# A decoder layer in five hand-ordered engine programs: first and last iterations as lists of their own, preparation in nine pieces, loads in another order

## The chip, the cores and the metric

The kernel runs on one core of one Trainium2 chip. The metric is the device time of one launch in microseconds (us), median of three runs. A TensorE clock share ("PEclk") of 1.00 is the full 2.4 GHz, 0.50 is 1.2 GHz.

## The reference

The inputs are x (32 batches of 256 tokens, 256 wide, float32), a context of the same shape and one cell number per token. The layer has three residual blocks, each ended by a layernorm:

```python
x = _layernorm(x + _L0_attn_ref(x, Wq, Wk, Wv, Wo), axis=-1)
x = _layernorm(x + _L0_xattn_ref(x, ctx, ctx, cell, ...), axis=-1)
x = _layernorm(x + _L0_ffn_ref(x, w_gate, w_up, w_down), axis=-1)
```

- Self-attention: 16 query heads and 4 key/value heads of 64, rotary embedding, scores of 256 x 256 with a linear position term, softmax, values, output projection Wo.
- Cross-attention: layernorms (with gain and bias) of x and the context, projections q, k, v, 16 heads of 16, each query window of 64 tokens against its own and the previous window, masked to earlier tokens of the same cell, softmax, values, another layernorm with gain and bias, output projection.
- FFN: activations rounded to 8 bits by the row's maximum, weights rounded to -1, 0, 1 times their mean magnitude, silu(gate) * up, rounded again, down projection.

## The kernel before

Five programs run side by side, one for each of SyncE (SP, all DMAs), TensorE (PE), VectorE (DVE), ScalarE (ACT) and GpSimd (POOL). Each batch's work is cut into some 90 **steps**. One list, `BODY` (line 66), gives the order of the steps for one iteration, each with a lag; in iteration `it` a step works on batch `it - lag` (lags 0 to 4), so work of up to five batches is mixed. Every engine walks through the same list and does its part of each step. Semaphores carry the dependences; their counts are worked out from batch and step (`at`, `landed`). `freed` gives what a step has to wait for before it may write its PSUM bank.

The main steps, by their names in the list (PE's part first, then what follows on other engines):

- `X`: x of a batch, transposed, is split into a rounded part x_hi (ACT, line 934) and a remainder x_lo (POOL, line 1019). `K`, `V`, `Q` project it (three matmuls for each product, line 364), DVE and POOL apply the rotation (lines 613 to 631, 1028). `kT`, `qT` transpose (line 352).
- `S` p (p = 0 to 7): scores of two heads (line 418); DVE adds the position term and takes the row maximum (line 641), ACT exponentiates (line 953), `R`: DVE's reciprocal (line 648) and POOL's normalisation (line 1037). `T` n (0 to 15): transposes of the probabilities (line 352), copied by ACT (line 960). `O` p: values (line 436). `W`: output projection (line 444); DVE adds x; `YS`: statistics and scaling.
- `NX`, `QX`, `QXT`: transposes of the normalised y, projection to the cross-attention's query `qx_tok` (line 370; DVE, then POOL at line 1060), transposes of it. `KP`, `VP`: keys and values from the transposed context `cT` (line 370), loaded by `load_ctxT` (line 305), which waits until KP and VP of the batch before have read it. `KXT` and `fill_kx` lay out the keys. `SX` s (0 to 3), `TX` s e, `OX` g: scores (lines 485, 492), exponentials (line 976), transposes and values (line 511). `BX`, `NO`, `PO`: back to tokens, output projection; `FS`, `X2`: layernorm (line 771).
- `QN`, `QC`, `XQ`, `G` n, `U` n, `HS`, `HC`, `HT`, `D`, `ZS`, `out`, `store`: FFN with its rounding, last layernorm (line 854) and the write of y.

Around the loop: SP increments 105 semaphores (line 282, all counters start above zero), then issues three first loads (the two halves of the projection weights and the rope table), then 15 more with all other constants, the FFN weights among them, and only then xT and the context of batch 0 (`run(0)`). DVE splits the projection weights into a rounded part and a remainder (lines 859, 862: four instructions). Each engine then does iteration 0, which holds batch 0's steps of lag 0 alone. Between iterations 0 and 1 stands the **preparation**: layernorm gains are multiplied into the cross-attention weights, their column means taken out and their biases turned into rows (lines 866 to 894, and matmuls at lines 577, 582 and following), the FFN weights' mean magnitudes and the three-valued weights are made (lines 868, 895 to 909), and `turned_bias` is copied (line 912). PE, ACT and POOL wait for `pre_dve`, a count of DVE's preparation instructions, before they go on to iteration 1. Iterations 1 to 4 are the fill, written out from the same list with the batches that don't exist left out; 5 to 31 are 27 rounds of a hardware loop; 32 to 35 are the tail, again from the same list.

```python
for it in range(FILL):
    run(it)
with act.Fori(0, LAST - FILL) as j:
    run(j + FILL)
for it in range(LAST, B + max(LAGS)):
    run(it)
```

Of the kernel before, what the change touches and what calls it, by code (L numbers as in the profile page):

```python
# [15 lines left out]
P = 128  # L16
# [39 lines left out]
    z_st=2, z_mv=2, z_eps=1, z_rstd=1, out_ready=1,  # L56
# [10 lines left out]
    (2, 'KXT'), (3, 'TX', 3, 1), (1, 'kT'), (4, 'out'), (0, 'load_xT'), (2, 'T', 13), (3, 'OX', 1), (1, 'S', 0),  # L67
    (2, 'R', 15), (1, 'R', 0), (3, 'BX', 0), (1, 'R', 1), (1, 'Q', 1, 2), (2, 'T', 14), (2, 'O', 6), (3, 'BX', 1),
    (3, 'OS'), (2, 'T', 15), (1, 'S', 1), (2, 'VP'), (2, 'O', 7), (1, 'T', 0), (1, 'R', 2), (3, 'NO'), (0, 'X'),
    (1, 'qT', 2), (1, 'T', 1), (3, 'PO'), (1, 'VC'), (3, 'FS'), (1, 'CS'), (1, 'load_ctxT'), (1, 'R', 3), (3, 'X2'),  # L70
    (3, 'QN'), (3, 'QC'), (1, 'S', 2), (2, 'W'), (3, 'XQ'), (2, 'YS'), (1, 'R', 4), (1, 'R', 5), (1, 'T', 2),
    (2, 'mask'), (0, 'K'), (2, 'NX'), (1, 'qT', 3), (3, 'G', 0), (3, 'U', 0), (1, 'T', 3), (1, 'S', 3), (1, 'O', 0),
    (1, 'load_xtok'), (1, 'load_cell'), (2, 'QX'), (1, 'R', 6), (3, 'G', 1), (3, 'U', 1), (3, 'HS', 0), (1, 'T', 4),
    (0, 'V'), (1, 'T', 5), (2, 'QXT'), (0, 'Q', 0, 1), (1, 'S', 4), (2, 'fill_kx'), (2, 'SX', 0), (3, 'HC', 0),
    (1, 'O', 1), (1, 'T', 6), (1, 'R', 7), (1, 'R', 8), (1, 'R', 9), (0, 'Q', 1, 1), (2, 'SX', 1), (1, 'KP'),
    (2, 'TX', 0, 0), (1, 'O', 2), (3, 'G', 2), (3, 'U', 2), (0, 'load_ctx'), (2, 'TX', 0, 1), (0, 'qT', 0),
    (1, 'T', 7), (2, 'TX', 1, 0), (3, 'G', 3), (3, 'U', 3), (2, 'load_vs'), (4, 'store'), (2, 'TX', 1, 1),
    (1, 'S', 5), (1, 'R', 10), (1, 'O', 3), (2, 'OX', 0), (1, 'T', 8), (3, 'HS', 1), (2, 'SX', 2), (0, 'qT', 1),
    (0, 'Q', 0, 2), (1, 'R', 11), (1, 'T', 9), (1, 'S', 6), (3, 'HT', 0), (3, 'HC', 1), (2, 'TX', 2, 0), (1, 'T', 10),
    (2, 'SX', 3), (1, 'O', 4), (3, 'HT', 1), (2, 'TX', 2, 1), (1, 'R', 12), (1, 'R', 13), (1, 'T', 11), (1, 'S', 7),  # L80
    (3, 'D'), (3, 'ZS'), (2, 'X1'), (1, 'R', 14), (1, 'O', 5), (2, 'TX', 3, 0), (1, 'T', 12),
]

# [26 lines left out]
def freed(sem, bank, step, it):  # L110
# [3 lines left out]
    while True:  # L114
# [8 lines left out]
        if it < 0:  # L123
            return sem[name], 1
# [1061 lines left out]
```

## Time and profile before

| | |
|---|---|
| median of 3 runs | 2415.59 us (2413.31 to 2416.63) |
| profiled execution | 2412.44 us |
| its span | 2410.6 us, granted clock 0.980 |
| PE busy | 2259.2 us (94%), 17643 instructions |
| DVE busy | 1878.8 us (78%) |
| ACT busy | 1554.5 us (64%) |
| POOL busy | 1220.5 us (51%) |
| loop, iterations 5 to 31 | 346.5 to 2231.4 us |

Busy times are shares of the whole span; they are averages over a start, a loop and an end with different limits, so the rows by stretch of time tell more than they do. The span begins with the first instruction; the run's time has 1.8 us around it. In the rows the TensorE clock is the mean of what was granted in the stretch.

### The profile page before, as it was taken

Reading aid. Unit: us, or ns where it says so; the run is one execution under the profiler, and the core shown is the slowest. Engines: PE = TensorE matmul, PEld = TensorE weight load, DVE = VectorE, ACT = ScalarE, POOL = GpSimd, SP = SyncE. Lnnn points to the kernel's source line nnn. Section 1 sums busy time; section 2 is a strip of 40 time slices with the busy share of each in tenths; the row PEclk is TensorE's granted clock in tenths of the full one; section 3 lists DMA queues with packets and bytes.
Section 4 is the critical chain, followed back from the end, with each engine's and each line's share of the span. In section 5 each row is a group of like instructions: output and inputs, shape, how many; then the busy total and the mean of one; then the engine's idle time right before and its main releaser. Section 6 shows DMA issues by size and latency. Waiting matters only on the chain. (4 is left out here: it accounts for less than half of the span.)

```text
span 2410.6 us, 61139 instructions
## 1 busy us (share of the span) xinstructions
PE 2259.2 (94%) x17643; PEld 1629.1 (68%) x17706; DVE 1878.8 (78%) x7997; ACT 1554.5 (64%) x4577; POOL 1220.5 (51%) x1422
## 2 busy tenths in 40 slices
PE   1589999999999999999999999999999999999974
PEld 1467777777776777777777777777777777677652
DVE  2656888888788888888888888788888878888765
ACT  0256676666667766667777666767666676776641
POOL 1254555555555555555554555555555555555421
PEclk9799999999999999999999999999999999999986
DMA  4010011111001111110011111001111100111000
GB/s 160 10 29 15 21 35 30 33 33 33 16 24 30 28 33 33 33 28 14 28 28 33 33 33 33 13 24 33 28 33 33 33 15 22 32 28 28 25 14 9
DMA packets 84439, 71.87 MB, mean 30 GB/s; under 512 B 18336, under 2 KB 79136, under 8 KB 84384
## 3 DMA queue, kind: packets, MB, share of 16 engines
q1 hardware_dynamic: 84384, 71.19, 10.4%
q8 instruction: 28, 0.46, 0.1%
q14 instruction: 27, 0.22, 0.0%
HBM read 45.98 MB, written 8.39 MB: 23 GB/s over the span
## 5 line engine op out<-in xcount | busy, mean ns | idle before, releaser
L953 ACT ACTIVATE prob<-prob,nmax 128x256 f32<-128x256 f32 x1024 | 508.7, 499 | 555.2 <-DVE nmax L641 555.2
L1037 POOL TENSOR_TENSOR prob<-prob,precs 128x512 f32<-128x512 f32 x512 | 524.5, 1040 | 455.3 <-DVE precs L648 455.3
L641 DVE CUSTOM_DVE_ANT_0 prob<-bank,alibi 128x256 f32<-128x256 f32 x1024 | 372.5, 420 | 103.7 <-PE bank L418 102.0
L976 ACT ACTIVATE px<-px,nmx 128x128 f32<-128x128 f32 x1024 | 313.2, 391 | 19.3 <-DVE nmx L733 19.3
L960 ACT COPY pT<-bank 128x512 f32<-128x512 f32 x512 | 299.1, 584 | 37.2 <-PE bank L352 32.0
L352 PE MATMUL bank<-ident,prob 128*128 128x128 f32 x2048 | 314.6, 276 | 7.2 <-ACT pT L960 4.7
L418 PE MATMUL bank<-kk,qq 64*128 64x256 f32 x2048 | 291.3, 403 | 0.9 <-ACT kk L941 0.9
L436 PE MATMUL bank<-pT,v_sb 128*64 128x256 f32 x2048 | 277.5, 392 | 1.8 <-ACT pT L960 1.8
L352 PEld LDWEIGHTS bank<-ident,prob 128*128 128x128 f32 x2048 | 235.7, 141 | 63.1 <-issue 27.0
L733 DVE CUSTOM_DVE_ANT_0 px<-bank,mask 128x128 f32<-128x128 f32 x1024 | 225.8, 285 | 14.7 <-PE bank L492 4.6
L444 PE MATMUL bank<-wo,oT 128*128 128x256 f32 x1024 | 229.5, 382 | 0.0
L364 PE MATMUL bank<-w_hi,x_hi 128*128 128x512 f32 (+1 forms) x512 | 190.7, 372 | 38.3 <-POOL x_lo L1019 34.6
L418 PEld LDWEIGHTS bank<-kk,qq 64*128 64x128 f32 x2048 | 176.7, 186 | 64.5 <-issue 48.7
L436 PEld LDWEIGHTS bank<-pT,v_sb 128*64 128x64 f32 x2048 | 124.1, 136 | 137.7 <-issue 97.8
L444 PEld LDWEIGHTS bank<-wo,oT 128*128 128x128 f32 x1024 | 192.0, 190 | 35.1 <-issue 10.3
L1028 POOL TENSOR_TENSOR qtok<-qtok,by_sin 128x512 f32<-128x512 f32 x128 | 163.5, 1277 | 103.1 <-DVE by_sin L631 102.9
L953 ACT ACTIVATION_READ_ACCUMULATOR prob<-prob,nmax 128x1 f32 x1024 | 193.5, 189 | 0.0
L364 PE MATMUL bank<-w_hi,x_lo 128*128 128x512 f32 (+1 forms) x512 | 173.8, 339 | 0.0
L364 PE MATMUL bank<-w_lo,x_hi 128*128 128x512 f32 (+1 forms) x512 | 173.7, 339 | 0.0
L352 PE MATMUL bank<-ident,px 128*128 128x128 f32 x1024 | 161.8, 281 | 4.7 <-ACT pTx L983 3.3
L983 ACT COPY pTx<-bank 128x512 f32<-128x512 f32 x256 | 149.6, 585 | 23.1 <-PE bank L352 23.1
L352 PEld LDWEIGHTS bank<-ident,px 128*128 128x128 f32 x1024 | 112.0, 142 | 51.7 <-issue 41.2
(187 smaller groups left out, 4404.7 us busy)
## 6 DMA issues: line engine op xcount, KB each, us to landing
xT<-in_xT SPq DMA_DIRECT2D x32, 256.0 KB, 2.8
ctxt<-in_ctx SPq DMA_DIRECT2D x32, 256.0 KB, 2.8
cT<-in_ctxT SPq DMA_DIRECT2D x32, 256.0 KB, 2.6
xtok<-in_x SPq DMA_DIRECT2D x32, 256.0 KB, 2.6
kx<-kxT SPq DMA_DIRECT2D x256, 32.0 KB, 2.0
vs<-vx SPq DMA_DIRECT2D x64, 128.0 KB, 2.8
out_y<-y SPq DMA_DIRECT2D x32, 256.0 KB, 2.6
cellk<-in_cell SPq DMA_DIRECT2D x32, 64.0 KB, 2.9
```

The costliest lines, as they stand in the source:

```text
L352: last = nc.tensor.transpose(bank[:, n * P:(n + 1) * P], src, ident[:])
L364: last = mm(to, xs[:, k, t * P:(t + 1) * P], ws[:, k, cols], start=i == 0, stop=i == KT * 3 - 1)
L418: last = mm(psum[SCORES[c]][:, q * L:(q + 1) * L], qq[half, u, m, q * P:(q + 1) * P], kk[half, p // 4, :], start=True, stop=True)
L436: last = mm(psum[bank][c * HD:(c + 1) * HD, 0:L], v_sb[:, k, g * HD:(g + 1) * HD], pT[:, p % 2, c, k, :], start=k == 0, stop=k == TT - 1)
L444: last = mm(psum[bank][:, t * D:(t + 1) * D], oT[:, k, t * P:(t + 1) * P], wo[:, k, :], start=k == 0, stop=k == PAIRS - 1)
L641: v.tensor_tensor_reduce(out=prob[:, (2 * p + q) % SLOTS, c, :], in0=psum[SCORES[c]][:, q * L:(q + 1) * L], in1=alibi[:, p % 2, c, :], sca ...
L733: v.tensor_tensor_reduce(out=px[:, s % 2, i, :], in0=psum[XSCORES[r]][:, h * P:(h + 1) * P], in1=mask[:, s % 2, :], scale=-1.0, scalar=3.0 ...
L953: nc.scalar.activation(prob[:, (2 * p + q) % SLOTS, c, :], prob[:, (2 * p + q) % SLOTS, c, :], ACT.Exp, bias=nmax[:, i:i + 1], scale=-1.0, ...
L960: nc.scalar.copy(pT[:, p % 2, :, :, q * P:(q + 1) * P].rearrange("p c k n -> p (c k) n"), bank[:].rearrange("p (c n) -> p c n", c=4)).then ...
L976: ins = nc.scalar.activation(px[:, s % 2, i, :], px[:, s % 2, i, :], ACT.Exp, bias=nmx[:, 8 * s + i:8 * s + i + 1], scale=-1.0)
L1028: g.tensor_tensor(qtok[:, t, :], qtok[:, t, :], by_sin[:, n % 2, :], ALU.add).then_inc(sem["rot_sum"], 1)
L1037: g.tensor_tensor(prob[:, n % SLOTS, :, :], prob[:, n % SLOTS, :, :], precs[:, 2 * n:2 * n + 2].unsqueeze(2).to_broadcast([P, 2, L]), ALU. ...
```

## The change

1. The list of steps is now three lists. `HEAD` gives all of iterations 0 to 4, with batch numbers in place of lags; `TAIL` all of 32 to 35; `BODY` is a new order for the loop, with lags that differ for some steps (XQ to G stay at 3; HT 1, D, ZS are at 4; VP stands ahead of KP of the next batch, six PE steps between them). `freed` goes by the place in the list.
2. The preparation is nine pieces ('prep', 0) to ('prep', 8) in `HEAD`. 0 are the four copies of the biases, 1 the bias matmuls, gain products and bias rows, 2 and 3 the turned biases and the centring, 4 `turned_bias`, 5 the sums of the FFN weights, 6, 7, 8 the three-valued weights, one matrix each. Piece 0 and 1 are ahead of batch 0's S 0, pieces 2 to 7 between its steps up to W, piece 8 behind its QXT.
3. SP issues its first loads, alibi among them, before the increments, then context and xT of batch 0, then the cross-attention constants ('loads', 0), Wo ('loads', 1) and, once the weights are split, the FFN weights ('loads', 2). These three groups have semaphores of their own.
4. The weights are split in twelve pieces of 512 columns. Staging buffers are other tiles (`pTx`, `hh`, `px`; `bwide` in `oT`).
5. DVE's X2 waits for y3_ready of the batch before, a wait that was not there.

```diff
 BODY = [
-    (2, 'KXT'), (3, 'TX', 3, 1), (1, 'kT'), (4, 'out'), (0, 'load_xT'), (2, 'T', 13), (3, 'OX', 1), (1, 'S', 0),
...
-    (0, 'V'), (1, 'T', 5), (2, 'QXT'), (0, 'Q', 0, 1), (1, 'S', 4), (2, 'fill_kx'), (2, 'SX', 0), (3, 'HC', 0),
...
+    (2, 'NX'), (3, 'G', 0), (3, 'U', 0), (2, 'QX'), (1, 'T', 4), (1, 'R', 7), (1, 'qT', 2), (3, 'G', 1), (3, 'U', 1),
+    (1, 'T', 5), (1, 'S', 4), (3, 'HS', 0), (3, 'G', 2), (1, 'O', 1), (3, 'U', 2), (1, 'T', 6), (0, 'V'), (1, 'R', 8),
+    (2, 'QXT'), (3, 'G', 3), (1, 'R', 9), (1, 'qT', 3), (3, 'U', 3), (1, 'T', 7), (1, 'S', 5), (2, 'fill_kx'),
+    (2, 'SX', 0), (1, 'O', 2), (0, 'Q', 0, 1), (2, 'VP'), (3, 'HC', 0), (1, 'T', 8), (1, 'R', 10), (1, 'CS'),
+    (1, 'R', 11), (2, 'TX', 0, 0), (2, 'SX', 1), (1, 'T', 9), (1, 'S', 6), (3, 'HS', 1), (1, 'O', 3),
+    (1, 'load_ctxT'), (1, 'KP'), (2, 'TX', 0, 1), (1, 'T', 10), (2, 'SX', 2), (1, 'O', 4), (2, 'TX', 1, 0),
...
+HEAD = [
+    (0, 'load_ctx'), (0, 'load_xT'), (0, 'loads', 0), (0, 'prep', 0), (0, 'loads', 1), (0, 'X'), (0, 'K'), (0, 'V'),
+    (1, 'load_xT'), (0, 'Q', 0, 1), (0, 'kT'), (0, 'Q', 1, 1), (0, 'CS'), (1, 'load_ctx'), (0, 'prep', 1),
+    (0, 'qT', 0), (0, 'qT', 1), (0, 'S', 0), (0, 'R', 0), (0, 'Q', 0, 2), (0, 'R', 1), (0, 'S', 1), (0, 'R', 2),
...
+    (0, 'R', 13), (0, 'S', 7), (0, 'R', 14), (0, 'KP'), (1, 'kT'), (0, 'T', 12), (0, 'T', 13), (0, 'R', 15),
+    (0, 'O', 5), (0, 'T', 14), (0, 'T', 15), (0, 'O', 6), (0, 'O', 7), (0, 'loads', 2), (0, 'prep', 5),
+    (0, 'prep', 6), (0, 'prep', 7), (1, 'S', 0), (1, 'R', 0), (0, 'VP'), (1, 'load_ctxT'), (0, 'load_xtok'), (0, 'W'),
...
+TAIL = [
...
+    (30, 'U', 0), (31, 'QX'), (30, 'G', 1), (30, 'U', 1), (31, 'QXT'), (31, 'mask'), (31, 'SX', 0), (31, 'TX', 0, 0),
+    (31, 'SX', 1), (31, 'VP'), (31, 'TX', 0, 1), (31, 'SX', 2), (30, 'G', 2), (30, 'U', 2), (31, 'load_vs'),
+    (30, 'HS', 0), (31, 'TX', 1, 0), (31, 'TX', 1, 1), (31, 'SX', 3), (30, 'HC', 0), (31, 'OX', 0), (31, 'TX', 2, 0),
...
+    (31, 'XQ'), (31, 'G', 0), (31, 'U', 0), (30, 'out'), (30, 'store'), (31, 'G', 1), (31, 'U', 1), (31, 'G', 2),
...
+def freed(sem, bank, part, n, it):
+    before = part[:n]
+    if part is BODY:
+        before = [(it - 1 - lag, *step) for lag, *step in BODY] + [(it - lag, *step) for lag, *step in before]
+    elif part is TAIL:
+        before = [(LAST - 1 - lag, *step) for lag, *step in BODY] + before
+    for batch, *step in reversed(before):
+        if holds(step[0], bank) or (step == ["prep", 5] and bank == 7):
...
         def _(sp):
+            for dst, src in first_loads:
+                sp.dma_start(dst, src).then_inc(proj_loaded, 16)
             for name, n in COUNT.items():
                 sp.sem_inc(sem[name], CREDIT * n)
...
+                    if kind == "loads":
+                        g, = args
+                        if g == 2:
+                            sp.wait_ge(pre_dve, W_SPLIT)
+                        for dst, src in later_loads[g]:
+                            sp.dma_start(dst, src).then_inc(later_loaded[g], 16)
...
+            def prepare(n, place):
+                crossed = (wkvx[:, :, 0:D], wqx, wkvx[:, :, D:2 * D], wox)
+                if n == 1:
+                    pe.wait_ge(later_loaded[0], 16 * len(later_loads[0]))
+                    pe.wait_ge(pre_dve, P_WIDE)
...
+                elif n == 5:
+                    pe.wait_ge(pre_dve, P_SUMS)
+                    pe.wait_ge(*freed(sem, 7, HEAD, place, 0))
+                    mm(psum[7][:, 0:3], ones, wsum[:], start=True, stop=True).then_inc(pre_pe, 1)
+                elif n == 8:
+                    pe.wait_ge(pre_dve, PRE_DVE)
...
+            def prepare(n):
...
+                elif n == 5:
+                    dve.wait_ge(later_loaded[2], 16 * len(later_loads[2]))
+                    for m in range(3):
+                        v.tensor_reduce(wsum[:, m:m + 1], stage[m], AX_X, ALU.add, apply_absolute_value=True).then_inc(pre_dve, 1)
...
                     elif kind == "X2":
+                        dve.wait_ge(*at("y3_ready", b - 1))
                         dve.wait_ge(*at("f_rstd", b))
...
-            for k in range(KT):
-                v.tensor_copy(w_hi[:, k, :], raw_w[k]).then_inc(pre_dve, 1)
...
+            for i in range(3):
+                cols = slice(512 * i, 512 * i + 512)
                 for k in range(KT):
+                    v.tensor_copy(w_hi[:, k, cols], raw_w[k][:, cols]).then_inc(pre_dve, 1)
...
-            run(0)
-            pool.wait_ge(pre_dve, PRE_DVE)
-            for it in range(1, FILL):
-                run(it)
+            run(HEAD)
```

How the instructions stand on three engines, before and in the change. First SP, from its first instruction. Before:

```order
L335 DMA hh<-in_wqkv 128x1536
L335 DMA pT<-in_wqkv 128x1536
L335 DMA rope<-in_rope 128x256
L337 DMA alibi<-in_alibi 128x1024
...
L337 DMA wo<-in_wo 128x8x256
...
L337 DMA brow<-in_b_o 128x256
L295 DMA xT<-in_xT 128x2x256
L301 DMA ctxt<-in_ctx 128x2x256
```

Now:

```order
L374 DMA hh<-in_wqkv 128x1536
L374 DMA px<-in_wqkv 128x1536
L374 DMA rope<-in_rope 128x256
L374 DMA alibi<-in_alibi 128x1024
L398 DMA ctxt<-in_ctx 128x2x256
L392 DMA xT<-in_xT 128x2x256
L389 DMA gb<-in_gb 128x16
L389 DMA wqx<-in_wqx 128x2x256
```

xT of batch 0 went from the nineteenth DMA to the sixth; the semaphore increments, which are no rows here, went from ahead of the first DMA to behind the fourth.

Then DVE, from batch 0's last projection step before its first score step (line 641 before, line 802 now). Before, with the rest of the preparation left out:

```order
L631 TENSOR_TENSOR by_sin<-bank,rope 128x8x32 x2
L866 COPY pTx<-gb 128x256 x4
L868 TENSOR_REDUCE wsum<-prob 128x1
L868 TENSOR_REDUCE wsum<-oT 128x1
L868 TENSOR_REDUCE wsum<-px 128x1
...
L909 TENSOR_SCALAR wd<-px 128x2048
L912 COPY turned_bias<-bank 128x512 x2
L641 ISA prob,nmax<-bank,alibi 128x256
```

Now:

```order
L792 TENSOR_TENSOR by_sin<-bank,rope 128x8x32 x2
L844 BN_STATS c_bn<-ctxt 128x6 x2
L848 BN_AGGR c_mv<-c_bn 128x2 x2
L706 TENSOR_SCALAR wkvx<-wkvx,gb 128x256 x2
L706 TENSOR_SCALAR wqx<-wqx,gb 128x256 x2
L706 TENSOR_SCALAR wkvx<-wkvx,gb 128x256 x2
L706 TENSOR_SCALAR wox<-wox,gb 128x256 x2
L708 TENSOR_TENSOR noT<-bank,noT 128x512
L708 TENSOR_TENSOR brow<-bank,brow 128x512
L802 ISA prob,nmax<-bank,alibi 128x256
```

Only piece 1 still stands between the projections and the first scores; the sums, centring and three-valued weights went behind them.

Last PE in the loop, around QXT, the transposes of qx_tok. Before:

```order
L352 MATMUL bank2<-ident,prob 128x128 x4
L352 MATMUL bank7<-ident,qx_tok 128x128 x4
L364 MATMUL bank3<-w_hi,x_hi 128x512
L364 MATMUL bank3<-w_hi,x_lo 128x512
L364 MATMUL bank3<-w_lo,x_hi 128x512
```

Now:

```order
L453 MATMUL bank3<-w_lo,x_hi 128x256
L441 MATMUL bank7<-ident,qx_tok 128x128 x4
L656 REGISTER_ALU
L658 MATMUL bank5<-wg16,xqT 128x512 x2
L522 REGISTER_ALU
L441 MATMUL bank4<-ident,qtok 128x128 x4
L668 MATMUL bank6<-wu16,xqT 128x512 x2
```

QXT stood behind two T steps and now stands behind V, with G 3, qT 3 and U 3 after it in place of a Q step.

## Rows read from the trace of the kernel before

**Rows 1.** Windows: us, then busy us (instructions) of PE, PEld, DVE, ACT, POOL; PEclk, DMA share, GB/s
```profile
0.00:34.60 34.60, 0.01 (x1) 0.04 (x1) 5.16 (x4) 1.90 (x2) 5.35 (x15) 1.00 0.72 252
34.60:53.60 19.00, 11.67 (x50) 8.67 (x50) 4.05 (x9) 1.78 (x3) 3.84 (x3) 0.93 0.16 48
53.60:63.70 10.10, 0.05 (x1) 0.01 (x1) 9.82 (x10) 0.00 (x0) 1.26 (x1) 0.50 0.00 0
63.70:93.20 29.50, 11.04 (x42) 8.76 (x42) 22.53 (x50) 0.00 (x0) 0.00 (x0) 0.73 0.00 0
95.00:154.70 59.70, 49.80 (x323) 34.26 (x323) 30.34 (x135) 37.10 (x115) 32.08 (x31) 0.97 0.05 14
346.50:2231.40 1884.90, 1871.69 (x14853) 1358.00 (x14906) 1552.70 (x6697) 1307.63 (x3862) 1026.81 (x1188) 1.00 0.10 28
2298.90:2361.00 62.10, 44.72 (x313) 28.71 (x314) 35.63 (x145) 22.42 (x55) 13.41 (x20) 0.84 0.06 14
2361.00:2410.60 49.60, 20.47 (x123) 11.00 (x124) 24.27 (x66) 4.51 (x7) 9.30 (x15) 0.61 0.03 11
```

**Rows 2.** Groups of SP's queue, line 330, at each loop end: first and last start
```profile
L330 SPq MOVE out_y<-y x27: 38/38/38, 385.4 to 2199.3; - x27
```

**Rows 3.** Start: groups (min/median/max ns), timeline (start, us, engine) and DMA issues
```profile
L282 SPq EVENT_SEMAPHORE  x105: 17/17/17, 0.7 to 7.3; - x105
...
25.54 0.43 SPq L295 DMA_DIRECT2D xT<-in_xT  x1
...
14.09 0.96 DVE L859 CAST w_hi<-hh 128x1536 fp32r<-128x1536 f32 x1 [14.09 <-DMA rope<-in_rope]
17.50 1.75 DVE L862 TENSOR_TENSOR w_lo<-pT,w_hi 128x1536 fp32r<-128x1536 f32 x1
...
32.37 0.62 ACT L934 CAST x_hi<-xT 128x512 fp32r<-128x512 f32 x1 [29.68 <-DMA xT<-in_xT]
...
xT<-in_xT SPq DMA_DIRECT2D x32, 256.0 KB, 2.8
alibi<-in_alibi SPq DMA_DIRECT2D x1, 512.0 KB, 6.5
```

**Rows 4.** Timeline of DVE in the preparation, first instruction for the three-valued weights
```profile
81.51 1.28 DVE L903 TENSOR_SCALAR prob<-prob,wrec 128x2048 f32<-128x2048 f32 x1
```

**Rows 5.** Last layernorm's scaling on DVE, its group; timeline of POOL at its first
```profile
L854 DVE TENSOR_SCALAR y<-y,z_mv,z_rstd x64: 407/651/670, 278.3 to 2407.7; 128x256 f32<-128x256 f32 x64
...
278.31 1.12 POOL L1054 TENSOR_SCALAR x<-y,y_negm,y_rstd 128x256 f32<-128x256 f32 x2
```

**Rows 6.** Timeline of PE's weight loads in one loop iteration
```profile
1052.53 0.47 PEld L352 LDWEIGHTS bank<-ident,prob 128*128 128x128 f32 x4
1053.16 0.73 PEld L418 LDWEIGHTS bank<-kk,qq 64*128 64x128 f32 x8 [0.17 <-issue]
1054.23 1.59 PEld L370 LDWEIGHTS bank<-wkvx,cT 128*128 128x128 f32 x8 [0.33 <-issue]
1056.15 0.63 PEld L436 LDWEIGHTS bank<-pT,v_sb 128*64 128x64 f32 x8 [0.33 <-issue]
...
1079.92 0.47 PEld L352 LDWEIGHTS bank<-ident,prob 128*128 128x128 f32 x4
1080.91 0.42 PEld L352 LDWEIGHTS bank<-ident,qx_tok 128*128 128x128 f32 x4 [0.52 <-POOL qx_tok L1060]
1081.29 0.19 PEld L364 LDWEIGHTS bank<-w_hi,x_hi 128*128 128x128 f32 x1
```

**Rows 7.** DMA issues: count, KB each, median us to landing
```profile
cT<-in_ctxT SPq DMA_DIRECT2D x32, 256.0 KB, 2.6
```

**Rows 8.** Timelines of PE and ACT: batch 31's SX 0, its second group's exponentials, OX 1
```profile
2331.27 2.08 PE L485 MATMUL bank<-kx,qx 64*128 64x512 f32 x4 [1.86 <-DVE qx L678]
...
2337.98 2.44 ACT L976 ACTIVATE px<-px,nmx 128x128 f32<-128x128 f32 x8 [1.67 <-DVE nmx L733]
...
2362.33 0.42 PE L511 MATMUL bank<-pTx,vx 128*32 128x128 f32 x8 [0.68 <-ACT pTx L983]
```

## Prediction of the change's time

> **What bounds the kernel now.** I read the windows by stage first [rows 1]. In the 27 loop iterations, from 346.5 to 2231.4 us, PE is busy 1871.69 of 1884.90 us, so the loop is bound by PE's own row of work; one iteration takes (2199.3 - 385.4) / 26 = 69.77 us by the loop-end marks [rows 2]. The ends are different. PE does nothing for the first 34.60 us. In 34.6 to 53.6 it projects batch 0. In 53.6 to 93.2, 39.6 us, the kernel prepares constants: PE is busy 0.05 + 11.04 us, ACT not at all, DVE 9.82 + 22.53 = 32.35 us, and the granted clock is 0.50 and then 0.73, the half-speed level (1.2 GHz) and a mixture with the full one. From 95.0, the first score step S0, to 154.7, where batch 0's W starts, PE is busy 49.80 of 59.70 us, DVE 30.34. At the other end, from 2298.9, PE is busy 44.72 of 62.10 and 20.47 of 49.60 us, at clocks of 0.84 and 0.61. So some 40 + 34 us at the start and 17 + 29 us at the end are waits that no PE work fills, and the loop has only 13 us of them. The change can win much at the ends, and in the loop only what PE loses between its instructions.
>
> **First part, loads and split.** The chain that ends the first wait is on SP. It makes 105 semaphore increments from 0.7 to 7.3, issues 18 DMAs, and only at 25.54 issues xT of batch 0; ACT's x_hi waits 29.68 us for it and starts at 32.37, and the first matmul comes at 34.60, 2.2 us behind x_hi's start [rows 1, 3]. Unqueued, an xT takes 2.8 us to land. Now the order has four DMAs first, then the increments, then ctxt and xT. The increments took 6.6 us, so xT is issued at about 0.7 + 6.6, plus some 2.7 for the five issues ahead of it (0.43 for one like it [rows 3], more for large ones), = 10.0, lands at 12.9, and x_lo is ready at 15.1. The weight split waits for alibi too: issued near 2.3, 6.5 us to landing, so 8.8; the split took from 14.09 to 17.50 + 1.75 = 19.25, 5.2 us, and I allow 0.7 more for the starts of eight further instructions, so it ends at 14.7. The first matmul goes to 15.1, bounds 14.7 (split alone) and 19 (xT queued behind the loads ahead of it: the old one was issued at 25.54 and landed only some 6.8 us later). Gain 19.5 us.
>
> **Second part, preparation.** Projections to S0 hold no preparation any more except pieces 0 and 1: 19.0 us of the old window, plus 93.2 to 95.0 (the kT step), less one projection of Q that now follows S0, about 3: 17.8 us. S0 comes at 15.1 + 17.8 = 33 instead of 95.0: -62 us. What was between must be done beside batch 0's attention. Of the 32.35 us on DVE, three ternary instructions of about 1.28 [rows 4], 3.8 us, are in the last piece, behind W; the other 28.5 us fall ahead of batch 0's W or ahead of S0. DVE is idle for 59.70 - 30.34 = 29.4 us of that stretch, so the bounds are 0 (all in idle time) and 28.5 (all on the path). The softmax of batch 0 runs in a chain through DVE, and the pieces are blocks of several microseconds that a score step must wait behind; but PE has 10 us of waits there already, and batch 1's projections now stand in them. I take 9, a third. The matmuls of the preparation, 11 us at a low clock, shrink towards 6 to 7 and are in PE's gaps. Start: -62 + 9 = -53 us.
>
> What DVE's pieces cost may be more than their old durations. The scaling of the last layernorm, two tensor_scalars of 128x256, took 407 ns each at the least and 651 at the median [rows 5]; and a POOL scaling starts at 278.31, at the same time as DVE's first at 278.3, so the longer ones are those beside POOL. Before, POOL had no instruction at all in the last 29.5 us of the preparation [rows 1]; now it normalises beside it. At 651 / 407 = 1.6, the tensor_scalars and copies in pieces 0, 1 and 8, about 8 us, would take 4.9 more; the ternary pieces 6 and 7 stand where POOL has little. All of it is in the 9 or hidden. The Trainium skill, page "SBUF — State Buffer", section "Who interferes with whom", says that DVE and GpSimd share one pair of ports under an exclusive lock, so that copies and tensor_scalars contend and reductions do not. That rule speaks against this change; with it added in full the sum would be 2324 instead of 2319, and the trace's 651 against 407 agrees with it.
>
> **Third part, the loop.** The steps are the same, so are the matmuls; only waits and the changes from one kind of step to another can differ [rows 6]. QXT (transposes of qx_tok) starts 0.99 us behind the transposes before it (1079.92 to 1080.91), where four transposes otherwise take 0.38 (1080.91 to 1081.29): 0.6 us of waiting for POOL's qx_tok. Between QX and QXT stood G1, U1, T4, V and T5; now also qT2, S4, G2, O1, U2 and T6 stand there, some 5 us more, so I count that as gone: -0.6. A step on the whole array ahead of one that uses half of its rows or columns costs 0.63 (1052.53 to 1053.16) instead of 0.38, so 0.25 more. The new list has 14 runs of such half-array steps instead of 15, and the two by-token steps VP and PO no longer stand directly in front of one (1.92 us from 1054.23 to 1056.15 for VP): -0.5. Against it stand places grown tight: NX to QX has only two FFN matmul pairs between, and G1 to G2 one transpose step, a score step and a tanh; +0.25. That makes -0.85 per iteration: 27 in the loop and 4 in the fill give 31 x -0.85 = -26 us. The bounds are 0 (each stall replaced by one of its size, 0.6 + 0.25) and -1.8 per iteration.
>
> VP and KP in the loop now share a short path: SP loads the next cT only when VP has read the last, and KP wants it. After VP's end come T8, TX, SX1, T9, S6 and O3: 0.38 + 0.63 + 0.63 + 1.07 (S, 1053.16 to 1054.23) and about 1 for each of SX1 and O3, some 4.7 us. A cT takes 2.6 us to land [rows 7] and 0.4 to issue: 1.6 us to spare. I cost it at nothing; the cover is those six steps. SP's queue is in order, but ahead of load_ctxT stand only fill_kx, long done by then.
>
> **Fourth part, the tail.** For the last batch PE goes from SX0 at 2331.27 to OX1 at 2362.33, 31.1 us [rows 8]. ACT's part in it is four groups of exponentials at 2.44 us and the copies, some 17 us; the rest is PE steps of FFN and waiting for scores that were asked for late. Now SX2 stands ahead of batch 31's OX0 and VP fills a gap, so I take 20: -11. The stretch ahead of W loses about 5. X2 of batch 31 now waits for y3 of batch 30, and out of 30 stands between U0 and U1: +2. Tail -14, bounds -4 and -24. Each list also holds other batches' steps than before (HEAD some 11 us less of PE, TAIL some 11 more); that cancels.
>
> **Sum.** -53 - 26 - 14 = -93 against the profiled execution of 2412.4: 2319.4. The median of the three runs, 2415.6, lies 3.2 above that execution; I give **2320**.
>
> **Rivals.**
> A, the forecast: 2303 to 2337. 0.59.
> B, the new loop order is better than counted: stalls and most changes of step vanish, 1.8 us per iteration; another 31 x -0.95 = -29: about 2291. For it: the loop's 0.7% idle is small, but weight loads show 0.1 to 0.5 us of stalls at many steps. Against: that is all that PE loses. 0.12.
> C, the loop gains nothing, each stall moved: +26, about 2346. For it: PE busy is 99.3%, so what a reorder can give is small and it may tighten others. 0.15.
> D, preparation pieces block the softmax chain of batch 0 to the full, made longer by POOL's traffic: 28.5 - 9 = +19.5 and up to 4.9: about 2341. For it: DVE makes each row maximum. Against: half of DVE's time there is idle. 0.08.
> E, slower than before: KP waits in each iteration for the cT that SP can issue only when VP is through. The start and tail win 67 us, so the loop would have to lose 2.5 us per iteration, on top of the 1.6 us to spare and of the 0.85 gained: the path VP, DMA, KP must be 5 us longer than 3.0 us, say because the landing takes 8 us beside the other loads. At 6 us of excess: -67 + 27 x 3.6 = +30, 2442. Nothing in the rows shows a cT so late. 0.04.
> F, the early S0 changes nothing later: batch 0 is waiting for the constants or for DVE until where it was, and the loop gives nothing: within 5 us of 2412. 0.02.
>
> **How the numbers follow.** The range takes in A to D: B's 2291 with its spread below, C's 2346 above: 2284 to 2350; outside are E, F and edges of B and D, some 0.15. About 0.2%, 4.8 us, is what a measurement of this kernel can tell from no change. Cases A to D are all faster by far more: 0.94; F is the same, 0.02; E slower, 0.04.
>
> **What would show it.** First matmul at 15 (19 would mean xT queued), S0 at 33, batch 0's W near 101, the loop entered about 67 us earlier (53, 3 of the fill's iterations, and the 11 of PE steps that went to the tail); loop period 68.9 by the loop-end marks; no wait of QXT on qx_tok; KP without a wait on cT; DVE's preparation pieces summing to 32 to 37 us; OX1 of the last batch some 20 us behind its SX0. I am wrong if S0 starts later than 40, if W(0) minus S0 is over 75 us (D), if the period is 69.7 or more (C) or below 68.3 (B), or if KP shows a wait of more than 1 us per iteration (E).

## The result and the profile after

The changed kernel takes **2455.54 us** (median of 4 runs, 2449.53 to 2456.05) against 2415.02 before: 1.0161 times as long, 95% interval 1.0146 to 1.0176. The forecast was 2320, with a range of 2284 to 2350 and 0.04 for slower. It was wrong in sign.

The windows by stage of the changed kernel, columns as in [rows 1]:

```profile
0.00:15.80 15.80, 0.00 (x0) 0.01 (x1) 5.71 (x12) 1.90 (x2) 5.78 (x15) 1.00 0.66 230
15.80:40.00 24.20, 15.70 (x64) 12.96 (x64) 7.48 (x24) 1.77 (x3) 4.83 (x5) 0.79 0.42 115
40.00:98.50 58.50, 49.80 (x316) 35.56 (x316) 44.97 (x144) 32.12 (x96) 27.23 (x25) 0.97 0.16 54
294.50:2273.10 1978.60, 1898.90 (x14906) 1392.20 (x14904) 1538.00 (x6699) 1319.67 (x3862) 1020.40 (x1186) 0.99 0.10 27
2403.00:2453.30 50.30, 24.16 (x132) 13.39 (x121) 26.52 (x75) 3.92 (x6) 8.56 (x15) 0.60 0.05 16
```

The first three rows are the start, and it went much as forecast: first matmul at 15.8 (34.6 before), S 0 of batch 0 at 40.0 (95.0), its W at 98.7 (154.7), with DVE busy 44.97 us of the last stretch instead of 30.34. The fourth row is the loop, and there the kernel lost: 1978.6 us for the same 27 rounds that took 1884.9, 79.7 us of them with PE idle, 13.2 before. The marks of the loop end give the period, as in [rows 2]:

```profile
L427 SPq MOVE out_y<-y x27: 29/29/29, 320.0 to 2228.3; - x27
```

(2228.3 - 320.0) / 26 = 73.40 us, against 69.77 before and 68.9 forecast.

To share the difference out I gave each PE step the shortest time that its kind took in the loop before, and compared the elapsed time of fill, loop and tail with the sum of the steps in them, since the three lists hold other steps than before. Beyond the steps' own time the fill took 132.9 us before and 90.9 after, -42.0; the loop 201.3 and 295.1, +93.8; the tail 81.1 and 71.9, -9.2. The sum, +42.6, is the difference of the spans but for rounding (2453.3 - 2410.6 = 42.7). PE's idle time, which needs no such account, says the same of the ends: 86.5 us before the loop and 43.9 after the change, 51.7 and 42.5 behind it.

Where the loop waits, the list of waits says only in part. The two that are new and large:

```profile
PE bank L441 <- ACT oT L1078: 58.8, 26, 2.7
DVE nmx L894 <- issue: 42.5, 26, 1.9
```

Line 441 is a transpose (here kT, which needs bank 4), line 894 the row maximum of SX. The first is 2.3 us per round, and was a wait that I had not looked for. The second is stranger: "issue" means that the engine waited for nothing that the profile shows. Here is the timeline of DVE at that place in one round, and ACT's behind it:

```profile
1248.16 0.27 DVE L809 RECIPROCAL precs<-psums 128x2 f32<-128x2 f32 x2 [1.37 <-ACT prob L1066]
1248.56 0.29 DVE L894 CUSTOM_DVE_ANT_0 px<-bank,mask 128x128 f32<-128x128 f32 x1
1250.67 0.08 DVE L894 DVE_READ_ACCUMULATOR2_ANT nmx<- 128x1 f32 x1 [1.82 <-issue]
1250.74 0.29 DVE L894 CUSTOM_DVE_ANT_0 px<-bank,mask 128x128 f32<-128x128 f32 x1
```
```profile
1247.65 0.58 ACT L1096 COPY pTx<-bank 128x512 f32<-128x512 f32 x1
1250.79 2.45 ACT L1089 ACTIVATE px<-px,nmx 128x128 f32<-128x128 f32 x8 [2.57 <-DVE nmx L894]
1253.14 0.35 ACT L1078 COPY oT<-bank 128x256 f32<-128x256 f32 x1
```

DVE stands still for 1.8 us between one instruction and the next one of the same SX 3. ACT's eight exponentials wait for it, ACT's copy of oT (O 5) is queued behind them, and kT on PE waits for that copy. SX 3 is the first thing in the new loop after three short ones. The page's list of DMA queues has the line that goes with it. After, and then before:

```profile
q14 instruction: 157, 1.29, 0.2%
```
```profile
q14 instruction: 27, 0.22, 0.0%
```

130 more packets of instructions, 5 for each of 26 rounds, each of 1.29 MB / 157 = 8.2 KB. In the trace they fall into the loop: round by round at -8.6, +1.0, +3.4, +5.8 and some +36 us from the branch at the end of DVE's loop. Before, there were none between the first round and the last. The same place shows what they cost. The loop's line, in the round above, has the branch back to its start (COMPARE_BRANCH) and the first register instruction that DVE runs behind it (FUSED_REGOPS):

```profile
L1030 DVEq COMPARE_BRANCH  x1: 68/68/68, 1245.1 to 1245.1; - x1
L1030 DVEq FUSED_REGOPS  x1: 74/74/74, 1248.0 to 1248.0; - x1
```

2.9 us lie between the two here, 2.85 in the mean of the 26 rounds; before, it was 0.28.

### The profile page after: what moved, and what is told of

Same layout as the page of the kernel before. It is cut to its first block and busy times, and to the rows that moved or that the text cites. A ratio compares the mean times of both kernels' runs of the same rounds, so it can differ in the third digit from the quotient of the medians.

```text
span 2453.3 us, 61410 instructions
## 1 busy us (share of the span) xinstructions
PE 2287.2 (93%) x17706; PEld 1662.5 (68%) x17706; DVE 1866.3 (76%) x8005; ACT 1568.6 (64%) x4577; POOL 1219.1 (50%) x1422
## 3 DMA queue, kind: packets, MB, share of 16 engines
q14 instruction: 157, 1.29, 0.2%
## 5 line engine op out<-in xcount | busy, mean ns | idle before, releaser
L441 PE MATMUL bank<-ident,prob 128*128 128x128 f32 x2048 | 320.1, 280 | 8.2 <-ACT pT L1073 7.0
L441 PEld LDWEIGHTS bank<-ident,prob 128*128 128x128 f32 x2048 | 243.4, 143 | 96.1 <-issue 55.7
L453 PE MATMUL bank<-w_hi,x_hi 128*128 128x512 f32 (+1 forms) x512 | 193.0, 377 | 23.7 <-POOL x_lo L1133 15.8
L441 PE MATMUL bank<-ident,px 128*128 128x128 f32 x1024 | 167.4, 288 | 18.3 <-ACT pTx L1096 15.6
L1207 POOL TENSOR_SCALAR hh<-hh,hs 128x1024 f32<-128x1024 f32 x64 | 71.7, 1121 | 212.2 <-DVE hs L987 212.2
```

The source lines that it names most:

```text
L441: last = nc.tensor.transpose(bank[:, n * P:(n + 1) * P], src, ident[:])
L453: last = mm(to, xs[:, k, t * P:(t + 1) * P], ws[:, k, cols], start=i == 0, stop=i == KT * 3 - 1)
```

## Theories

**F, loading of instructions:** DVE's loop doesn't stay in the engine's instruction buffer and is loaded again in each round, because of where in the program it begins. DVE's program has 974 instructions ahead of a loop of 339 before, and 951 ahead of 340 after. **O, the order:** the new order of the steps is worse by itself; it puts ACT's copy of O 5 behind the exponentials of SX 3. The forecast's own rival for "slower", a late cT, was out at once: PE has no wait on cT.

## Experiments

**1. More instructions ahead of DVE's loop**, 64 of them.

```diff
+            for _ in range(64):
+                dve.sem_inc(waits_passed, 1)
             dve.wait_ge(proj_loaded, 16 * len(first_loads))
```

> The changed kernel with 64 more instructions at the very start of DVE's program (semaphore increments that nobody waits for, made while DVE waits for the loads), nothing else. In the trace of the change, queue q14 moved 157 packets of instructions where before it moved 27, 130 more, 5 for each of 26 loop rounds, and DVE stands still for 1.2 us at its loop end and for 1.55 to 1.9 us behind the first instruction of SX 3 with no wait to blame. Theory F (DVE's loop is loaded anew in every round, because of where in the program it begins; before it began elsewhere): q14 falls back to about 27 packets, both stalls are gone, the wait of kT for bank 4 shrinks from 2.5 to about 0.8 us, the period goes from 73.3 to 71.5 or a little lower, the time to about 2405. Theory O (the order of the new loop is to blame: the copy of O 5 stands behind the eight exponentials of SX 3 on ACT): period stays at 73.3 within 0.3 us and the time at 2455, even if q14 falls.

Measured: 2404.23 us, 0.9957 of the kernel before (0.9938 to 0.9975), 51 us less than the change, by instructions that do nothing. The stall behind the maximum was gone and the period fell to (2176.7 - 320.6) / 26 = 71.39. But q14 did not fall:

```profile
q14 instruction: 158, 1.29, 0.2%
```

so the theory was right about what costs, wrong about what the 64 had done, and the time came out as expected (2405) by luck. The loads were all still there, and so was the stall at the branch, 2.91 us in the mean; the second one, behind the maximum, was gone. The profile shows the first as a wait at the reciprocals, 43.1 us in 26 rounds, 1.66 each.

**2. The same in the kernel before**, with 190 in place of 64.

> The kernel before with 190 such instructions at the start of DVE's program, which shift its loop by 190 places. Theory F: by the number of instructions ahead of the loop (974 before, 951 in the change, loops of 339 and 340) the shifted loop again begins late in a block; q14 goes from 27 to about 157 packets, DVE stands still twice per round for 1.2 and some 1.6 us. If DVE's start of the loop matters there as in the change, the time rises by 1 to 3 us per round, 2440 to 2490; if those stalls fall into DVE's idle time, it stays at 2415 though q14 shows 157. Theory O: q14 at 27 or 157 makes no difference, 2415 within 5 us.

Measured: 2488.98 us, 1.0306 (1.0280 to 1.0332), 74 us more than the kernel before with the same steps in the same order. Some 7 us of it come ahead of the first loop end (392.5 instead of 385.4): DVE is busy with the 190 until 19.18 and splits the weights 5.1 us later. The loop has the rest, a period of (2279.1 - 392.5) / 26 = 72.56. Its waits and its queue:

```profile
DVE kxT L713 <- issue: 78.0, 26, 3.2
PE bank L511 <- DVE kxT L713: 59.0, 26, 2.5
```
```profile
q14 instruction: 159, 1.30, 0.2%
```

The first DVE instruction of the old loop, kxT of line 713, now comes 3.0 us late in 26 rounds, and PE waits 59.0 / 26 = 2.3 of them (2.5 at the most). From the branch to the first register instruction it is 2.88 us, where the same loop had 0.28. Theory O can't explain this run, since the order is the old one.

**3 and 4. O 5 ahead of SX 3**, without and with 64 instructions.

```diff
-    (2, 'R', 13), (2, 'R', 14), (3, 'TX', 1, 1), (3, 'SX', 3), (2, 'O', 5), (2, 'load_xtok'), (2, 'T', 12),
+    (2, 'R', 13), (2, 'R', 14), (3, 'TX', 1, 1), (2, 'O', 5), (3, 'SX', 3), (2, 'load_xtok'), (2, 'T', 12),
```

> The changed kernel with one step moved in the loop: O 5 of lag 2 stands directly ahead of SX 3 of lag 3 instead of behind it, so ACT copies oT ahead of the eight exponentials and bank 4 is free for kT when PE comes to it. Theory O: the wait of kT (2.22 us per round more than the step before it took elsewhere) is gone, period 73.3 to about 71.1, time about 2395. Theory F: the stall of DVE is still there and PE waits at the next step that needs SX 3's exponentials (TX 2 or TX 3) or the probabilities, so a part comes back: period 71.5 to 73.3, time 2405 to 2455, q14 at 157.

Measured: 2442.95 us, 1.012 (1.0093 to 1.0147): 12.6 us less than the change, 0.5 per round, where theory O wanted 2.2. The wait of kT was not the cause, only the place where DVE's stall came out; taken away, the stall came out elsewhere. From 400 to 2100 us DVE still stood still for 1.6 us per round behind SX 3's first instruction, and a transpose now waited for DVE's by_sin instead, 1.8 us per round:

```profile
PE bank L441 <- DVE by_sin L792: 41.9, 23, 2.1
```

> Both edits: 64 instructions ahead on DVE and O 5 ahead of SX 3. If the two stalls are one chain (fetch delays SX 3's maxima, these ACT, this kT), the two together give hardly more than the better of them, period about 70.7 to 71.3. If they are separate, they add: period near 69.3, time about 2345. The gain that was forecast for the loop (68.9) would need both and nothing else in the way.

Measured: 2398.48 us, 0.9934 (0.991 to 0.9958), 5.8 us below run 1, less than half of the 12.6 that the same move gave without the 64. The two don't add, as for one chain.

**5. Thirty instead of sixty-four.** Four places were now known, three with loads and one without. They fit one rule: a block, one packet, is 128 instructions, and a loop stays in the buffer if it touches no more than three of them. A loop of 340 must then begin at place 0 to 44 of a block. How many instructions of start-up stand ahead of what the program shows isn't known; the four places fit the rule if it is 54 to 72. The kernel before then begins at 4 to 22, the change at 109 to 127, run 1 at 45 to 63 and run 2 at 66 to 84. Thirty more put the change at 11 to 29. So far this is one unknown fitted to four places, and this run is its first test.

> The changed kernel with 30 instructions ahead on DVE instead of 64. In the two shifted runs q14 still moved 158 and 159 packets, and their times in the trace show blocks of 8 KB being loaded 4 to 5 times per round; with 64 the stall behind SX 3's first instruction was gone, one of 1.54 us at DVE's loop end stayed. Theory F, sharpened: a block is 128 instructions of 64 B, DVE keeps four, and the loop of 340 is held only where it touches three of them and the fourth is for what is loaded ahead; the kernel before (no load in the loop, 974 + its start-up) and the three others bound the start-up to 50 to 69 instructions, so 30 more put the loop's start 8 to 26 into a block. Expected: no load of instructions in the loop, q14 at 27 to 29, no stall at DVE's loop end, period 71.35 down to between 70.4 and 71.2, time 2378 to 2400. If the rule is wrong: 158 packets and a time of 2404 or more. Theory O (what is left over 69.8 is the order): the period stays above 70.2 even with no load.

Measured: **2367.16 us**, 0.9809 (0.9786 to 0.9831), better than both kernels, better than the 2378 to 2400 expected, and 88.4 us below the change. The page's line, the loop's branch, and DVE at its loop's start:

```profile
q14 instruction: 28, 0.23, 0.0%
```
```profile
L1032 DVEq COMPARE_BRANCH  x1: 56/56/56, 1134.5 to 1134.5; - x1
L1032 DVEq FUSED_REGOPS  x1: 74/74/74, 1134.8 to 1134.8; - x1
```
```profile
1135.45 0.69 DVE L874 TENSOR_TENSOR kxT<-bank,turned_bias 128x512 f32<-128x512 f32 x1
1136.06 0.25 DVE L809 RECIPROCAL precs<-psums 128x2 f32<-128x2 f32 x2
1136.59 0.29 DVE L894 CUSTOM_DVE_ANT_0 px<-bank,mask 128x128 f32<-128x128 f32 x1 [0.28 <-PE bank L610]
1136.80 0.08 DVE L894 DVE_READ_ACCUMULATOR2_ANT nmx<- 128x1 f32 x1
```

From the branch to the first register instruction it is 0.28 us in the mean, as in the kernel before. From kxT's start to the first maximum's read-out it is 1.35 us; in the change it was 4.6 (1246.11 to 1250.67). So the 1.37 us that the change's profile put down to ACT at the reciprocals was a stall for instructions too: the reciprocal of 1248.16 stands right behind the register instruction of 1248.0. Loop: 1890.0 us, period (2140.2 - 320.2) / 26 = 70.00.

**6. The same with O 5 first.**

> The same 30 instructions and O 5 ahead of SX 3 in the loop. With 64 the move gave 0.2 us per round. Theory F: no load in the loop, 0.2 below the period of the run without the move: 70.2 to 71.0, time 2373 to 2394. Theory O would have the order's waits here too; if kT's wait for bank 4 was what the order cost (about 1.0 us per round with 64), the period is 0.8 lower than without the move.

Measured: 2372.94 us, 0.9833 (0.981 to 0.9855), period 70.23, q14 at 28. Without the loads the moved step is a loss of 5.8 us; in run 4 it had been a gain of the same size.

**7. New ends, old loop.** HEAD cut by (3, 'KXT') and filled up with 18 steps in the old order from (3, 'load_xtok') to (3, 'T', 12), TAIL likewise, `BODY` the old one.

> The changed kernel's HEAD, TAIL, preparation, loads and split, but the old order of steps in the loop; HEAD is cut and filled up to what the old loop expects (one step of it left out, 18 put behind in the old order), TAIL likewise (18 left out, one put ahead). DVE's loop then begins at 985 instead of 951, which by the rule of blocks needs no shift: no load in the loop, q14 27 to 29. Period as before, 69.8; the fill's gain of 42 and the tail's of 9 stay, less up to 8 for the junctions: time 2415 - 51 = 2364, up to 2372. That would say that the new order of the loop brought nothing and that all of the change's gain is in its ends. If the ends' gain hung on the new loop's order, the time would be above 2385.

Measured: 2375.99 us, 0.9844 (0.9821 to 0.9867), q14 at 28, period (2169.9 - 355.7) / 26 = 69.78, the old one. The loop of run 5 is some 5 us longer than this one's in all, while its fill, measured beyond the steps' own time, is 12.5 us shorter. I put that down to my junction of two orders, dearer than the 8 allowed; no run shows it apart from the order of the fill itself. So the new order of the loop costs some 5 us, and all that the change wins is in its ends.

**8 and 9. Preparation pieces 0 and 1 later**, in run 7's and in run 5's kernel. Run 8, shown here, puts piece 0 directly ahead of piece 1; run 9 puts both behind Q 1 2, the last projection.

```diff
-    (0, 'load_ctx'), (0, 'load_xT'), (0, 'loads', 0), (0, 'prep', 0), (0, 'loads', 1), (0, 'X'), (0, 'K'), (0, 'V'),
+    (0, 'load_ctx'), (0, 'load_xT'), (0, 'loads', 0), (0, 'loads', 1), (0, 'X'), (0, 'K'), (0, 'V'), (1, 'load_xT'),
...
+    (0, 'Q', 0, 1), (0, 'kT'), (0, 'Q', 1, 1), (0, 'CS'), (1, 'load_ctx'), (0, 'prep', 0), (0, 'prep', 1),
```

> As the run before it, with preparation piece 0 (DVE's four copies of the biases, which wait for all ten loads of the cross-attention's constants) put from ahead of batch 0's K directly ahead of piece 1. In the trace of the change DVE waits 8.4 us for the last of these loads with K's rotation queued behind it, and PE 6.4 us for the rotation's bank; S 0 of batch 0 comes at 40.0 where 33 was forecast. Expected: that wait gone, S 0 at 33 to 35, the time 5 to 7 us lower than the run before it. If the preparation's products are what S 0 waits for, or the later stages take it back: within 2 us of it.

Measured: 2378.71 us (2375.17 to 2379.52), 0.9856; no gain. Q 1 1 came at 28.4 instead of 31.9, S 0 at 40.9 instead of 38.8: PE now waited 3.7 us for piece 0's copies ahead of the bias matmuls of piece 1.

> The changed kernel with 30 instructions ahead on DVE (2367.2 us) and preparation pieces 0 and 1 moved in HEAD from ahead of batch 0's first scores to behind its last projection Q 1 2. Putting piece 0 alone later freed the projections (Q 1 1 at 28.4 instead of 31.9) but S 0 stayed at 40.9, so what S 0 waits for would be piece 1: DVE's copies and eight products, which hang on the last load. Expected if so: S 0 at 33 to 35 (the forecast's 33), the fill 5 to 7 us shorter, time 2360 to 2362. If batch 0's stretch has no room for the 7 to 8 us of DVE's two pieces, they come back before W of batch 0: time within 2 us of 2367.

Measured: 2370.71 us, 0.9816 (0.9799 to 0.9833), 3.5 us more than run 5. S 0 did come at 33.6, the forecast's 33; but S 2 came at 53.1 instead of 50.2, and the 3 us stayed to the end. The bias matmuls of piece 1 took them. PE had stood idle for 3.6 us, waiting for DVE's copies, and then ran these matmuls from 44.7 to 51.4, at a granted clock of 0.54 in 44.6 to 51.3, nearly all of it at the half-speed level; in run 5 they ran from 34.9 to 38.5 at 1.00. One of the groups, in run 9 and in run 5:

```profile
L470 PE MATMUL bank<-wqx,oT x4: 634/634/634, 46.5 to 47.8; 128*128 128x256 f32 x4
L470 PE MATMUL bank<-wqx,oT x4: 379/379/379, 35.7 to 36.4; 128*128 128x256 f32 x4
```

All sixteen take 6.7 us instead of 3.6, and S 2 stands behind them. The expectation that the move would be worth 5 to 7 us was wrong, and so was the alternative of an even exchange.

**10. The order of the loads alone**, in the kernel before.

```diff
         def _(sp):
+            for dst, src in first_loads:
+                sp.dma_start(dst, src).then_inc(proj_loaded, 16)
             for name, n in COUNT.items():
...
-            for dst, src in first_loads:
-                sp.dma_start(dst, src).then_inc(proj_loaded, 16)
+            run(0)
             for dst, src in flat_loads:
                 sp.dma_start(dst, src).then_inc(weights_loaded, 16)
-            for it in range(FILL):
+            for it in range(1, FILL):
```

> The kernel before with only SP's order changed: the three first loads ahead of the semaphore increments, xT and context of batch 0 ahead of the other constants (alibi stays with those; the split stays in four instructions, the preparation where it was). DVE's program is unchanged, so no load of instructions in the loop and a period of 69.8. Expected: first matmul from 34.6 to about 14 to 16, and what follows moves with it as long as the constants have landed; they are issued from about 11 to 28 and the last must land by 53.6 - 19 = 34.6. Then the time is 17 to 19 us lower, 2395 to 2398, and of the fill's 42 us the other 23 are the preparation's. If the constants or the FFN weights are late, only 5 to 15 us are won.

Measured: 2394.07 us, 0.991 (0.9887 to 0.9934), 21 us less; in the profiled executions 18. First matmul at 14.02, S 0 at 79.8 instead of 95.0, first loop end at 369.3 instead of 385.4, 16.1 earlier. Of the fill's 42 us the loads make 16. The rest is what the preparation between the steps and the new order of the fill bring together; no run takes these two apart. The first matmul is even 1.8 us earlier than in the change, for xT is issued at 8.78, ahead of context and alibi, and at 10.15 there.

**11. 158 instead of 30.**

> The changed kernel with 158 instructions ahead on DVE, 128 more than the 30 that took the loads out of the loop. Theory F with blocks of 128: the loop begins at the same place in a block as with 30, so again 27 to 29 packets on q14, period 70.0, time 2365 to 2370. If it is the length of the way or something else that the 30 happened to hit: loads come back (157), time 2400 or more. The extra semaphore increments run while DVE waits for the loads, at most 2 us are added at the start.

Measured: 2367.67 us, 0.9803 (0.9785 to 0.9822), q14 at 29, period 70.01. A whole block more changes nothing: what counts is the place in a block of 128.

The blocks can also be seen in the trace, without any rule. Outside the loop, one series of q14's packets starts when DVE has executed 195, 324, 448, 579, 706, 833, 962, 1094 and 1220 instructions in the kernel before, some 128 apart. With 158 idle instructions ahead (run 11) it has 193, 322, 448, 574, 705, 830, 965, 1094 and 1214: the blocks stay where they are in the program, and the loop moves over them. Most of the packets between them follow ACT's count (55, 176, 304, 444, 580, 707), so q14 isn't DVE's alone; but the 130 in the loop came and went with instructions that only DVE had. If a packet starts as DVE enters a block, the boundary near 194 puts the start-up at some 62, inside the 54 to 72: an estimate, but one that doesn't use the loop.

## Why the prediction was wrong

**The loop.** The step that failed reads "The steps are the same, so are the matmuls; only waits and the changes from one kind of step to another can differ". The steps are the same; where they begin in DVE's program isn't. That made 88 us of the loop's +94 (run 5 against the change), 3.4 us per round (73.40 - 70.00). None of the rivals had it. E was right that a new wait per round could turn the sign, but named a transfer of data, and its turning point of 2.5 us net stood on ends that win 67; they won 51, so 1.9 would do. The Trainium skill, "Runtime: NRT & Kernel Launch", section "Instruction fetch mechanics", says that a taken branch to a place outside the pages that an engine holds stalls it while they are fetched. The trace agrees, with 2.85 us from the branch to the next instruction of the loop where it is loaded and 0.28 where it isn't. Read as a question to this loop, it would have been the rival that ends slower. The size of its pages doesn't fit what q14 shows here: it has pages of 256 instructions and two of them, 512, held; with these, run 1 would begin its loop at place 45 to 63 of 256, stay within two pages and have no loads. It had 158 packets, of 8.2 KB. No other length of start-up helps. With such pages the starts that load would be 83 in a row out of every 256, but 951 and 1015 load, 64 apart, and 974, 981 and 985 between them don't. By the runs, the blocks are of 128 and a loop must stay within three.

**The loop's own gain** was forecast as 0.85 us per round and is -0.2 (70.0 in run 5, 69.8 before). PE's weight loads in run 5, around QXT and around KXT:

```profile
1180.67 0.57 PEld L441 LDWEIGHTS bank<-ident,prob 128*128 128x128 f32 x4
...
1182.63 0.46 PEld L441 LDWEIGHTS bank<-ident,qx_tok 128*128 128x128 f32 x4
1183.15 0.12 PEld L658 LDWEIGHTS bank<-wg,xqT 128*128 128x128 bf16 x2
...
1132.44 0.73 PEld L536 LDWEIGHTS bank<-kk,qq 64*128 64x128 f32 x8 [0.17 <-issue]
1133.62 0.42 PEld L441 LDWEIGHTS bank<-ident,kx_tok 128*128 128x128 f32 x4 [0.44 <-issue]
1134.68 0.42 PEld L441 LDWEIGHTS bank<-ident,px 128*128 128x128 f32 x4 [0.64 <-ACT pTx L1098]
```

QXT's wait on qx_tok is gone, as counted. But T 5, which had carried it, now stands ahead of a score step and takes 0.74 instead of 0.99, so 0.25 of the 0.6 remained as gain. KXT now has TX 1 1 behind it, which waits for ACT's copy out of bank 3: 1.06 us instead of 0.5. And transposes such as T 2 and BX 0 that took 0.39 take 0.64, since each now stands ahead of a step on half the array. I had counted runs of half-array steps, 15 and 14, and the two dearest neighbours; not what stands ahead of each. By the two lists the new order has transposes directly ahead of such a run 12 times, the old one 10 times. That counting was worth 0.5 in the sum; with two more of the 0.25, and the wait of KXT, nothing of it is left in the period.

**The first loads** were right: 15.8 for 15.1, 18.8 us gained for 19.5.

**S 0** was not: 40.0 for 33. This is the second step that failed. The sentence "Projections to S0 hold no preparation any more except pieces 0 and 1" costed them at nothing. Piece 0 waits for all ten loads, and K's rotation is queued behind it on DVE:

```profile
22.88 0.90 DVE L701 COPY oT<-gb 128x256 f32<-128x256 f32 x4 [8.44 <-DMA brow<-in_b_o]
23.70 0.68 DVE L774 TENSOR_TENSOR ktok<-bank,rope 128x512 f32<-128x512 f32 x1
```

Run 9 shows that S 0 can come at 33.6, and that it did not help. The forecast's -62 also took work that is put off for work that is saved. PE was busy for 23.9 us ahead of S 0 before and for 15.7 after, so of the 55 us that S 0 came earlier, 8.2 had still to be done; PE's idle time ahead of S 0 fell by 46.8 (71.1 to 24.3). The 40 us of preparation that the forecast called waits had 11 us of PE's work in them as well.

**Preparation beside attention**, +9, was 0 by its own measure: from S 0 to W of batch 0 it took 58.7 us with it, 59.7 without. A part of the price came later: from S 0 to the loop PE was idle for 19.6 us, 15.4 before, most of the difference between the W of batch 0 and that of batch 1 (8.4 for 4.5). Pieces 6 and 7 hold DVE while batch 1's softmax waits, and POOL with it:

```profile
106.44 1.04 POOL L1151 TENSOR_TENSOR prob<-prob,precs 128x512 f32<-128x512 f32 x1 [15.25 <-DVE precs L809]
```

But PE was busy for 13.37 of the 15.20 us from 91.2 to 106.4, so this wait alone can have cost no more than 1.8. At W of batch 0 the change was 56 us ahead, at the loop's start 52, with some 10 us of PE's steps moved to the tail: 42 by the account above, for 53 plus 3 forecast. The forecast had the loop entered 67 us earlier.

**Contention of DVE and POOL** (up to 4.9 us) did not occur in these pieces: the scaling instructions of piece 1 take 345 ns each, as before, and the large ones of pieces 6 and 8:

```profile
L755 DVE TENSOR_SCALAR pTx<-pTx,wrec x1: 1287/1287/1287, 96.6 to 96.6; 128x2048 f32<-128x2048 f32 x1
L755 DVE TENSOR_SCALAR px<-px,wrec x1: 1283/1283/1283, 124.8 to 124.8; 128x2048 f32<-128x2048 f32 x1
```

against 1.28 in [rows 4]. POOL was idle beside them: in the 15.25 us above, and in 124.8 to 128.6 by its window. The sentence "now it normalises beside it" was wrong, since POOL normalises what DVE hands it. Where a copy does meet POOL, the trace agrees with the rule that was weighed there (the Trainium skill, "SBUF — State Buffer", section "Who interferes with whom": one of the two waits for the other's whole instruction). The kernel before has such a case among its four copies of the biases:

```profile
L866 DVE COPY pTx<-gb x4: 279/280/1370, 55.0 to 56.7; 128x256 f32<-128x256 f32 x4
```

The one of 1370 ns runs from 55.22 to 56.59, beside POOL's rotation of q from 55.18 to 56.44; in the change, with POOL idle, none of the four takes more than 293. In run 9, where they are beside POOL again, one takes 1347.

**The tail** gave 9 of 14. From SX 0 to OX 1 of the last batch it takes 25.1 us (2377.1 to 2402.2), where 31.1 had been and 20 was taken.

**The sum** without the loads: -93 forecast, -46 measured (spans, 2364.9 in run 5 against 2410.6). Even then the 2367 would lie outside the range: the loop's 27 rounds gave +5 for -23, the fill -42 for -56, the tail -9 for -14.

## What to carry to other kernels

Before trusting a reordered hardware loop, look at the page's count of instruction packets and compare it with the kernel before: a handful per loop round means that an engine reloads its loop, and a number of idle instructions ahead of the loop, tried in steps, tells what that costs. The distance from the loop's branch to the first instruction behind it shows the stall even where the list of waits blames another engine. Compare two orders of a loop only with both free of it; run 4 and run 6 gave opposite signs for the same move. What a step costs in a dense row depends on the step behind it, so a change in order is to be summed over every neighbour pair, not over the conspicuous ones.

## What the hardware showed beyond the forecast

- A loop of 339 to 340 instructions on DVE ran without loading instructions when it began at (974, 981, 985, 1109) instructions of the program, and loaded 5 packets of 8.2 KB per round when it began at 951, 1015 or 1164. Two starts 128 apart behaved alike. That the buffer holds four such blocks, one for what is loaded ahead, is my reading of these seven places; other lengths of a loop were not tried.
- The stall at the branch was nearly the same in every run with loads, 2.85 to 2.94 us in the mean, against 0.28 or 0.29 in those without. Its price was not: by the periods 3.4 us per round in the change, where a second stall of 1.6 stands behind it, 2.8 in run 2 and 1.4 in run 1.
- The profile names this stall "issue", or puts it down to an engine that DVE was no longer waiting for (ACT at the reciprocals).
- Sixteen fp32 matmuls of 128x128 by 128x256 took 6.7 us where PE had waited 3.6 us and the granted clock was then 0.54, and 3.6 us at 1.00 (runs 9 and 5).
